# Six graph layers over 64 graphs on one core: how the biases and the 19 weight matrices are split into two halves of float16 before and between the first graphs

## Time and profile before

| | us |
|---|---|
| median of 3 runs (lowest, highest) | 3245.1 (3242.33, 3245.72) |
| the profiled execution | 3241.71 |
| its span, first to last instruction | 3240.0 |
| PE busy in the span | 3094.3 (96%) |
| DVE busy | 2712.0 (84%) |
| ACT busy | 1666.2 (51%) |
| POOL busy | 482.7 (15%) |

### The profile page before, as it was taken

The page is one execution under the profiler, slowest core; times in us unless marked ns, Lnnn a source line. Parts: engine busy times, 40 slices in busy tenths (PEclk is TensorE's granted clock), DMA queues, the critical chain, the costliest instruction groups (busy, mean ns, idle before and its releaser), DMA issues.

```text
span 3240.0 us, 86317 instructions
## 1 busy us (share of the span) xinstructions
PE 3094.3 (96%) x34944; PEld 2413.3 (74%) x34944; DVE 2712.0 (84%) x7670; ACT 1666.2 (51%) x4446; POOL 482.7 (15%) x908
## 2 busy tenths in 40 slices
PE   0799999999999999999999999999999999999996
PEld 0477777777777777777778777777777777777774
DVE  6588888888888888888888888888888888888885
ACT  3255555555555555555555555555555555555553
POOL 1111111111111111111111111111111111111110
PEclk9999999999999999999999999999999999999997
DMA  5000000000000000000000000000000000000000
GB/s 165 7 8 13 13 8 13 13 7 13 13 7 13 13 7 13 13 7 13 13 7 13 13 7 13 13 10 11 13 13 7 13 13 7 13 13 7 13 7 6
DMA packets 36979, 47.73 MB, mean 15 GB/s; under 512 B 3668, under 2 KB 36564, under 8 KB 36584
## 3 DMA queue, kind: packets, MB, share of 16 engines
q1 hardware_dynamic: 36544, 42.15, 4.1%
q10 hardware_dynamic: 40, 0.06, 0.0%
HBM read 29.62 MB, written 12.58 MB: 13 GB/s over the span
## 4 chain that ended last, share of the span: by engine, by line
PE 94%; DVE 2%; ACT 2%; issue 1%; DMA 1%; POOL 0%; ACTq 0%; POOLq 0%; SPq 0%; DVEq 0%
PE bank_a L266 27%; PE bank_c L266 22%; PE bank_b L266 20%; PE bank_c L310 7%; PE bank_b L297 4%; PE bank_c L438 3%; PE bank_b L304 2%; PE bank_b L310 2%; PE bank_c L454 1%; PE bank_c L453 1%; PE bank_c L455 1%; ACT htc_hi L559 1%; PE bank_a L343 1%; PE bank_b L392 1%; PE bank_a L310 1%
## 5 line engine op out<-in xcount | busy, mean ns | idle before, releaser
L573 ACT ACTIVATE prob<-score,neg_head_max 128x128 f32<-128x128 f32 x1536 | 495.0, 393 | 22.4 <-DVE neg_head_max L828 21.8
L266 PE MATMUL bank_c<-htc_hi,w_lo 128*128 128x128 f16 x2304 | 409.0, 219 | 0.0
L266 PE MATMUL bank_c<-htc_hi,w_hi 128*128 128x128 f16 x2304 | 409.0, 219 | 0.0
L266 PE MATMUL bank_c<-htc_lo,w_hi 128*128 128x128 f16 x2304 | 409.0, 219 | 0.0
L266 PE MATMUL bank_a<-w_hi,hta_hi 128*128 128x384 f16 x1152 | 377.0, 328 | 0.0
L266 PE MATMUL bank_a<-w_lo,hta_hi 128*128 128x384 f16 x1152 | 376.9, 327 | 0.0
L823 DVE SCALAR_TENSOR_TENSOR score<-bank_c,bias 128x384 f32<-128x384 f32 x512 | 279.9, 547 | 55.7 <-PE bank_c L438 55.5
L828 DVE TENSOR_REDUCE neg_head_max<-score 128x3 f32<-128x384 f32 x512 | 279.4, 546 | 8.9
L621 DVE SCALAR_TENSOR_TENSOR pt_lo<-bank_c,pt_hi 128x384 f16<-128x384 f32 x512 | 271.2, 550 | 18.6 <-ACT pt_hi L497 18.6
L310 PE MATMUL bank_c<-ident,prob 128*128 128x128 f32 x1536 | 245.1, 276 | 9.5 <-ACT prob L573 9.1
L497 ACT ACTIVATE pt_hi<-bank_c 128x384 f16<-128x384 f32 x512 | 239.9, 482 | 24.9 <-PE bank_c L310 24.9
(11 more groups left out here) (185 smaller groups left out, 8886.4 us busy)
## 6 DMA issues: line engine op xcount, KB each, us to landing
x_in<-x SPq DMA_DIRECT2D x64, 192.0 KB, 2.4
out<-y_out SPq DMA_DIRECT2D x64, 192.0 KB, 2.3
w_stage<-w_t SPq DMA_DIRECT2D x10, 576.0 KB, 5.7
adj_in<-adj SPq DMA_DIRECT2D x64, 64.0 KB, 2.2
score<-w_t SPq DMA_DIRECT2D x5, 576.0 KB, 5.5
prob<-w_t SPq DMA_DIRECT2D x4, 576.0 KB, 7.1
norms<-norm_rows SPq DMA_DIRECT2D x8, 192.0 KB, 5.0
m_sides<-biases ACTq DMA_DIRECT2D x5, 6.0 KB
```

The lines of the kernel that those rows point to most:

```text
L266: mm = nc.tensor.matmul(out_ap, a, b, start=first and i == 0, stop=last and i == len(pairs_of) - 1)
L573: ex = nc.scalar.activation(prob[:, j, c, :], score[:, j, c, :], ACT.Exp, bias=neg_head_max[:, j, c:c + 1])
```

## The change

Biases: one DMA of ACT loads all 20 rows to 20 partitions (row r on partition r, in the tile self_part). ACT makes the high part of all in one instruction into pt_hi, DVE the low part in one into pt_lo, and two DMAs of ACT spread them, the high part to partition 0 of bias_hl and the low part to partition 1. PE waits for b_spread 32 rather than for ten pieces.

Weights: SP loads only the first four matrices, and right behind them the norm rows. ACT issues the other 15 loads itself, one ahead of each high part from matrix 1 on (for matrix m that of m + 3, after a wait for the low part of m - 1). The matrices 0, 1 and 2 are split before the streams begin; the other 16 are split between steps of the streams, at the places of the table SPLITS: on ACT and on DVE after the letter at the (period, place) given. For graph 0 PE waits for the first matrix of a layer (A and B) and later for the rest of them.

The orders: ORDER and FIRST of all four engines are new too. PE takes two probability transposes earlier in both halves of the period, turn_adj (d) ahead of the last context of layer A1, the transpose of attn_a in A0 earlier; ACT copies attn_ta ahead of self_part in A1; DVE does the step of delta_b and attn_b earlier; POOL makes the masks of layer A at the start of its period.

```diff
-B_PIECES = (N_W + 1) // 2
+W_FIRST = 3
 ORDER = {
-    "pe": "xcxxyybayyyayyyxcbxwbwwccwcwcwccaccadcayyyyyyyyawcbwxxxxcxxxwcbxcwcxbccccbwacwyybaxxxx",
-    "act": "bbcabaccbxccwcppcppwwacacccabcbbcpbwcpcbpwpxbpabbwc",
-    "dve": "aaqacaaabbacabnaaabacccccbcbcbbcbpjpppjjjpjaaaacamaaipiiicainccbccczccpczbbzpbnbppapbbabbp"
-           "bappppbanp",
-    "pool": "aabcanlqbbm",
+    "pe": "xcxxyybayyyayyyxcbxwbwccwwcwccwcaccdacayyyyyyyyawcbwxxxxcxxxcwbcxcxwccbccabcwcwyybaxxxx",
+    "act": "accbxccwpcpcpwpawccaccabcbcpbbpccpbpwxwbapbbwcbbcab",
+    "dve": "aaacbbabnabaaqaacccccbcbcbbcbpjpppjjjpjaaacaapaiaiimicainccbccczccpczbpbpbzbpaapbbbbpbapnp"
+           "nppbapaaca",
+    "pool": "lbaabcanqbm",
 }
...
+SPLITS = {
+    "act": [(0, 36), (0, 40), (0, 44), (0, 44), (0, 49), (1, 7), (1, 13), (1, 16),
+            (1, 19), (1, 19), (1, 22), (1, 23), (1, 28), (1, 29), (1, 36), (1, 40)],
+    "dve": [(1, 94), (1, 94), (1, 96), (2, 2), (2, 8), (2, 12), (2, 15), (2, 15),
+            (2, 40), (2, 47), (2, 54), (2, 59), (2, 59), (2, 59), (2, 73), (2, 78)],
 }
...
         @block.sync
-            for m in range(N_W):
-                if m >= W_STAGES:
-                    sp.wait_ge(w_hi_split, m - W_STAGES + 1)
-                    sp.wait_ge(w_lo_split, m - W_STAGES + 1)
...
+            for m in range(W_STAGES):
+                sp.dma_start(w_stage[m], w_t[m, :, :].rearrange("(c p) n -> p c n", p=128)).then_inc(w_loaded[m], 16)
+            for i in range(8):
+                sp.dma_start(norms[:, i, :], norm_rows[i:i + 1, :].to_broadcast([128, D])).then_inc(norms_loaded, 16)
...
         @block.scalar
+            def split_high(m):
+                n = m + W_STAGES - 1
+                if W_STAGES <= n < N_W:
+                    act.wait_ge(w_lo_split, m)
+                    act.dma_start(w_stage[n % W_STAGES], w_t[n, :, :].rearrange("(c p) n -> p c n", p=128))\
+                        .then_inc(w_loaded[n % W_STAGES], 16)
                 act.wait_ge(w_loaded[m % W_STAGES], 16 * (m // W_STAGES + 1))
...
+            act.dma_start(b_rows, biases[:, :]).then_inc(b_loaded, 16)
+            act.wait_ge(b_loaded, 16)
+            nc.scalar.activation(b_hi, b_rows, ACT.Copy, scale=W_SCALE).then_inc(b_hi_split, 1)
+            act.wait_ge(bias_zeroed, 1)
+            act.wait_ge(b_hi_split, 1)
+            act.dma_start(bias_hl[0:1, :, :], b_hi).then_inc(b_spread, 16)
+            act.wait_ge(b_lo_split, 1)
+            act.dma_start(bias_hl[1:2, :, :], b_lo).then_inc(b_spread, 16)
+            for m in range(W_FIRST):
+                split_high(m)
...
         @block.vector
+            dve.wait_ge(b_hi_split, 1)
+            lo_part(b_lo, b_rows, b_hi, W_SCALE).then_inc(b_lo_split, 1)
+            for m in range(W_FIRST):
+                split_low(m)
```

More of the change, by code:

```diff
@@ L27 @@
     "pe": {"a": (0, 4), "b": (1, 3), "c": (2, 10), "d": (1, 0), "w": (0, 6), "x": (1, 5), "y": (2, 8)},
[3 rows of a table removed]
[3 rows of a table added]
+}
+SPLITS = {
[3 more added lines that the diff above has]
+            (2, 40), (2, 47), (2, 54), (2, 59), (2, 59), (2, 59), (2, 73), (2, 78)],
 }
@@ L196, in gnn_stack_kernel @@
         w_hi_split, w_lo_split = sem("w_hi_split"), sem("w_lo_split")
-        b_loaded = [sem(f"b_loaded{i}") for i in range(2)]
-        b_hi_split, b_rest, b_split, b_pick = sem("b_hi_split"), sem("b_rest"), sem("b_split"), sem("b_pick")
+        b_loaded, b_hi_split, b_lo_split, b_spread = sem("b_loaded"), sem("b_hi_split"), sem("b_lo_split"), sem("b_spread")
         bias_zeroed = sem("bias_zeroed")
@@ L206, in quad, with woven @@
             return (layer - 4) * QUADS + j + 1
-        def bias_rows(piece):
-            return (m_sides, qk)[piece % 2][0:2, :, :, :].rearrange("p c s n -> p (c s n)").rearrange("p (b d) -> p b d", d=D)
-        def woven(engine, **streams):
+        b_rows = self_part[0:N_W + 1, :]
+        b_hi, b_lo = (of[0:N_W + 1, 0, :, :].rearrange("p c n -> p (c n)") for of in (pt_hi, pt_lo))
+        def woven(engine, splits=None, **streams):
             order, first = ORDER[engine], FIRST[engine]
@@ L217, in woven @@
                 seen = dict.fromkeys(streams, 0)
-                for letter in order:
+                for place, letter in enumerate(order):
                     if (period, seen[letter]) >= first[letter] and letter in live:
@@ L222, in woven @@
                     seen[letter] += 1
+                    for _ in range(SPLITS.get(engine, []).count((period, place))):
+                        next(splits)
                 period += 1
@@ L316, in weights @@
                     pe.wait_ge(w_lo_split, W_INDEX[layer] + last + 1)
-                    pe.wait_ge(b_split, B_PIECES)
+                    pe.wait_ge(b_spread, 32)
                     pe.wait_ge(dve_consts, 4)
@@ L352, in weight_a @@
                     k, m = l + 1, W_INDEX[l]
-                    weights(g, l, 2)
+                    weights(g, l, 0)
                     pe.wait_ge(*hta_lo_ready.at(g, k))
@@ L358, in weight_a @@
                     yield
+                    weights(g, l, 2)
                     pe.wait_ge(*expo_a_ready.at(g, k))
@@ L401, in weight_b @@
                     k, m = l + 1, W_INDEX[2 + l]
-                    weights(g, 2 + l, 2)
+                    weights(g, 2 + l, 0)
                     pe.wait_ge(*htb_hi_ready.at(g, k))
@@ L411, in weight_b @@
                     yield
+                    weights(g, 2 + l, 2)
                     pe.wait_ge(*htb_full_ready.at(g, k))
@@ L587, in turned_c, with later_weights @@
                         yield
[L589 to L604, removed]
-                act.wait_ge(w_loaded[m % W_STAGES], 16 * (m // W_STAGES + 1))
-                nc.scalar.activation(w_hi[:, m, :, :], w_stage[m % W_STAGES], ACT.Copy, scale=W_SCALE)\
-                    .then_inc(w_hi_split, 1)
+            def split_high(m):
[4 more added lines that the diff above has]
+                        .then_inc(w_loaded[n % W_STAGES], 16)
+                act.wait_ge(w_loaded[m % W_STAGES], 16 * (m // W_STAGES + 1))
+                nc.scalar.activation(w_hi[:, m, :, :], w_stage[m % W_STAGES], ACT.Copy, scale=W_SCALE).then_inc(w_hi_split, 1)
+            def later_weights():
+                for m in range(W_FIRST, N_W):
+                    split_high(m)
+                    yield
+            act.dma_start(b_rows, biases[:, :]).then_inc(b_loaded, 16)
[7 more added lines that the diff above has]
+            for m in range(W_FIRST):
+                split_high(m)
             def stream(steps):
@@ L611, in stream @@
                     yield from steps(g)
-            woven("act", a=stream(chain_a), w=stream(weight_a), b=stream(chain_b), x=stream(weight_b),
+            woven("act", later_weights(), a=stream(chain_a), w=stream(weight_a), b=stream(chain_b), x=stream(weight_b),
                   c=stream(chain_c), p=stream(turned_c))
@@ L896, in _, with split_low, later_weights @@
             V.memset(v_hi[:, :, HEAD:HEAD + 1], 1.0).then_inc(dve_consts, 1)
[L897 to L907, removed]
+            def split_low(m):
                 dve.wait_ge(w_hi_split, m + 1)
                 lo_part(w_lo[:, m, :, :], w_stage[m % W_STAGES], w_hi[:, m, :, :], W_SCALE).then_inc(w_lo_split, 1)
+            def later_weights():
+                for m in range(W_FIRST, N_W):
+                    split_low(m)
+                    yield
+            dve.wait_ge(b_hi_split, 1)
+            lo_part(b_lo, b_rows, b_hi, W_SCALE).then_inc(b_lo_split, 1)
+            for m in range(W_FIRST):
+                split_low(m)
             def stream(steps):
```

3 lines of the change are left out of this document (2 added, 1 removed), and 6 rows, old and new, of the table FIRST.

## The result

The changed kernel takes 3185.3 us (median of 4 runs, 3184.5 to 3186.1); the kernel before took 3243.7 beside it. The ratio is 0.982 [0.981, 0.983], a gain of 58 us where 53 were forecast. The profiled execution took 3186.1 us with a span of 3184.3, against 3241.7 and 3240.0 before: 55.7 us of span to explain.

The account below looks back on a forecast made before the run. PE sets the pace once all layer pairs run; at the start the bias and weight queues hold it. 3241.7 - 66.8 + 19.1 + 2 - 6.8 = 3189.2, with 3.4 to the median 3192.6, said as 3192; range 3180 to 3203 (0.57).

Parts of the forecast that it names:

- Start: Ahead of PE's first turn: bias pieces go, three matrices split first, PE starts at 19.4 instead of 86.20 us, -66.8 us.
- Rival (e): At the start: PE's first turn waits for something else, such as loads landing together at about 12 us; +4, no chance given.
- The 16 later matrices: In the ramp: splits between steps delay the turns of A1, B0, B1 and C0 by 3.7, 14.6, 21.2 and 19.1 us.
- the term for the clock: In the ramp: longer idle stretches put more of PE's matmuls at the lower clock, +2 us taken, between 0 and 14.
- W5: Split of matrix 5, ahead of bn_stats in the ramp: delays it by 2.4 us, less what lies in parallel.
- W13: Split of matrix 13, ahead of node_b's normalization: +4.3 us, its high part waiting for graph 1's exponential.
- rival (a): In the ramp: the splits hide in idle time, 3169 us (3166 to 3180), chance 0.15.
- The 14 us: In the ramp: the clock's upper bound, all of PE's 28.9 us cold and half of it on the chain.
- Rival (b): The ramp costs more, by the clock (+14 instead of +2) or a late load: 3204, up to 3212, chance 0.13.
- The full periods: turn_adj ahead of A1's context saves 0.11 us a period, 62 times: -6.8 us, between 0 and -16.
- (c): A new wait of 0.2 to 0.5 us in each period, by T1 or a copy: 3204 to 3223, chance 0.12.
- Rival (d): Slower than before: a quad's exponentials 0.98 us late against T1 in both halves of each period, 3258, chance 0.03.

Follow-up runs that it names:

- run 1: The kernel before with only the new biases (one load, one high and one low part, two spreading DMAs): 3206.6 us, ratio 0.989.
- run 2: The changed kernel with the old ten pieces of biases, so only the weights and orders changed: 3222.1 us, ratio 0.993.
- run 4: The changed kernel with PE's turn_adj (d) put back behind the context of layer A1, one letter of the order: 3190.6 us, ratio to before 0.984.
- run 3: The kernel before with only the new ORDER and FIRST of all engines: 3236.7 us, ratio 0.997.
- run 8: The changed kernel with SP issuing the later weight loads and splits moved to places where the engines had time: 3166.1 us, ratio 0.976.
- run 7: The changed kernel with 590 dummy 128x128 matmuls in PE's idle stretches of the first graphs: 3182.5 us.
- run 6: The changed kernel with SP instead of ACT issuing weight loads 4 to 18, split places unchanged: 3180.8 us.
- run 5: The changed kernel again, unedited, as the measure for two other runs on one chip: 3186.1 us.
- run 9: The changed kernel with one place moved, ACT's high part of W13 ahead of graph 1's exponential: 3184.9 us.
- run 10: The kernel of run 8 with W_FIRST = 0, the first three matrices also split behind the first turn: 3162.0 us, ratio 0.974.

## Why the prediction was right

**The bound.** As read: PE's work is the same to 0.1 us, and all of the gain is time ahead of its stream (66.3 us) and between its matmuls (5.3), less what the ramp took (15.9).

**Start.** Forecast -66.8, measured -66.3. Runs 1 and 2 give it as 34.5 for the biases and 31.8 for the weights, two queues in a row whose parts add up. The rows that had to bear the sum, the changed kernel on ACT and then DVE:

```profile
7.31 0.85 ACTq L614 DMA_DIRECT2D bias_hl<-pt_hi  x1
8.20 0.72 ACTq L616 DMA_DIRECT2D bias_hl<-pt_lo  x1
8.97 1.16 ACT L602 ACTIVATE w_hi<-w_stage 128x1152 f16<-128x1152 f32 x1 [5.48 <-DMA w_stage<-w_t]
...
12.01 1.16 ACT L602 ACTIVATE w_hi<-w_stage 128x1152 f16<-128x1152 f32 x1 [1.87 <-DVE w_lo L632]
```

```profile
16.21 1.36 DVE L632 SCALAR_TENSOR_TENSOR w_lo<-score,w_hi 128x1152 f16<-128x1152 f32 x1 [1.65 <-ACT w_hi L602]
```

The first high part began 0.6 us later than I took, and not for the reason that I had. The row names the load, but the load of W0 was issued at 3.59 and landed 4.9 us later, at 8.5; ACT came free only at 8.20 + 0.72 = 8.92. The two issues of the biases took 0.85 and 0.72 us where I had 0.37 each, behind the memset of bias_hl. So the start goes through the memset and these two issues, with the load 0.4 us behind the lead (in run 4 the load landed at 9.1 and was the last). The three pairs took 16.21 + 1.36 - 8.97 = 8.6 us (8.7 forecast), and from there to PE it was again 2.3. That the first turn came within 0.5 us of the forecast with the wrong step in front is in part luck. Rival (e) did not come about.

**The 16 later matrices.** The mechanism was right and the terms too large: 19.1 for the steps and 2 for the clock, where the two together measured 15.9 (17.3 against run 3, which has the same orders and no split in the ramp). The turns came 17.85, 45.0, 64.4 and 83.25 us behind the first, against 18.1, 47.0, 67.4 and 86.4 without the term for the clock. How the surplus lies between these turns is known only roughly, because they scatter: with the same splits at the same places runs 2 and 4 had B0 at 44.0 and 43.8 and C0 at 82.9 and 83.0. DVE waited for ACT's high part at every place that I had named (W5, W7, W9 to W11, W13), and also at W4, W8, W14, W15, W17 and W18. W5 was sized right: the context ended at 32.15 + 0.62 = 32.8 and stats_a began at 35.13, 2.4 us later, as forecast. W13, which I had as the dearest at +4.3, cost 2.8 (run 8 against the changed kernel). Its high part had to wait for the exponential of graph 1, as I had it: ACT stood ready for 4.00 us until DVE's row maximum released the exponential. Which part of the 4.3 was too high is not known, and of the overpriced splits only W13 was isolated. How the missing 5.2 us divide between the steps and the clock stays open, since run 7 does not bound the clock.

**What the ramp costs is place, not work.** This was rival (a), "the splits hide in idle time", and my reason against it was that a queue in order can't fill a gap that it doesn't reach. For the table as it is, that held. Run 8 shows that it is a property of the table and of the loads behind ACT's wait: the same 16 pairs, at other places and with SP issuing, cost nothing that can be told from the scatter (0.03 us against the orders without any). Run 6 gives the loads' share as 3.7 of the 16; whether the new places would do it with ACT issuing was not tried.

**The clock.** The granted clock did fall, to 0.76 in the windows from 40 to 80 us, between the levels of 1.2 and 2.4 GHz, behind waits of PE of up to 5.63 us. The Trainium skill, in TensorE: Matmul & The Clock Gate, "HAM oscillation — how this bites in real kernels", says that idle gaps between bursts put the array back to half rate, and the trace of the changed kernel agrees. A long gap was not needed for it in run 7: the block of A1 shown there was slow behind waits of no more than 0.91 us. The 14 us did not come: with the clock of the windows held near 1.00 the turn of B1 came 3.8 us sooner and that of C0 2.2, some of it from stretches that were slow in the kernel before too. Whether the 2 was too much or too little is not shown, because two blocks stayed slow in run 7. At these places PE mostly waits for other engines; that this is why the slow clock is cheap is argued from the windows, not shown by itself. Rival (b) did not come about.

**The full periods.** Forecast -0.11 us a period by turn_adj; the period fell by 0.10, and one letter is 0.08 of it (run 4). The wait for htc_hi was not touched by it. All the waits of PE between 1000 and 2000 us are the same as before, 5.4 us in 21 places:

```profile
PE bank_c L270 <- ACT htc_hi L565: 5.4, 21, 0.3
```

No wait for prob: rivals (c) and (d) had margins of 0.2 us against them and these held. (Rival (d) takes the exponentials' end as 1546.06 where the earlier trace rows give 1546.00; no row shows the 0.06, which is 4 us in its 3258.) The rest fell by 5.3 and not 6.8, since the periods behind graph 28 gained less: (3240.0 - 1505.08) - (3184.3 - 1451.82) = 2.4 us for more than half of the graphs.

**The sum and the median.** The forecast of the span was nearer than its terms: the start gained 0.5 us less than forecast and the full periods 1.5 less, while the ramp cost 5.2 less, which leaves 3.2. That these cancel in part is luck. Of the 7.3 us by which the forecast of 3192.6 was high, 3.1 is this sum (3189.2 against 3186.1); 3.4 is the step from the profiled execution to the median, which I took to stay, and 0.8 is that the changed kernel's median stands below its profiled run. The step belonged to the scatter of the kernel before, and that scatter went with the change (below).

## What to carry to other kernels

Work moved from ahead of a pipeline into its ramp was free here only where its two halves (ACT's and DVE's) stood at places that both engines reach at about the same time, and nothing urgent stood behind them; busy shares of 40 to 65% on each engine did not say that it is so. Give the loads of such work to a queue that has nothing else to wait for. When two serial preparations are taken off the start, price them separately: here they added up to 0.1 us. Then follow the chain of the start again: once both were gone, it went through a memset of 6.5 us on POOL and the two DMA issues behind it.

## What the runs showed that I had not expected

- The same load of 576 KB landed in 3.8 to 4.0 us (median) when ACT issued it singly in the ramp, against 5.5 to 7.1 us for the kernel before, where one load stood close behind another. No high part of the ramp waited for its load. That the spacing is what made the loads faster was not tried by itself.
- Scatter. Every kernel with the new orders, the changed one and runs 2 to 10, ranged over 0.2 to 2.8 us between its executions. The kernel before ranged over 8.8 us in thirteen runs and run 1, with the old orders, over 7.1 in four. So it goes with the orders; with which step of them was not tried. In the thirteen runs the mean granted clock goes with it: 0.994 in the spans up to 3239.8 us, 0.993 between and 0.992 from 3244.2 us on; what moves it is not known. The scatter is also why run 3 gains 9.3 us by medians and 5.1 by spans.
- The memset of bias_hl, unchanged by the edit, is hidden in neither kernel. In the kernel before ACT's first bias piece waited 3.71 us for it; in the changed kernel it stands ahead of the two issues that end at 8.92; in run 10 it stands ahead of the first root. How much a shorter one would gain was not tried: in the changed kernel the load of W0 lands only 0.4 us before ACT comes free.
